# Attention with a relation bias and a mixture of experts: the relation part of the scores moved to 64-row tiles

## The chip, the cores and the metric

One core of a Trainium2 chip runs the kernel. The metric is device time in microseconds, the median of several runs; less is better.

## The reference, cut to what matters

One layer on 4096 tokens of width 256, 16 heads of width 16, then a mixture of 8 experts, two a token. The change is in the attention; its scores have an unusual term, a softmax over three relations for every pair of tokens, gated by the query.

```python
q, k, v = (x @ W.T + b).reshape(b, s, h, hd)          # for Wq, Wk, Wv
attn_scores = einsum('bihd,bjhd->bhij', q, k) / scale
logits = (x @ rel_W[:, :d].T)[:, :, None, :] + (x @ rel_W[:, d:].T)[:, None, :, :] + rel_b
relation_probs = softmax(logits, axis=-1)             # three relations per pair (i, j)
bias = einsum('bijk,hk->bhij', relation_probs, logical_bias)
gate = sigmoid(x @ gate_W.T + gate_b)                 # per query and head
attn_weights = softmax(attn_scores + gate * bias, axis=-1)
out = einsum('bhij,bjhd->bihd', attn_weights, v).reshape(b, s, d) @ Wo.T + bo
x = x + out
x = x + mixture_of_experts(layernorm(x))
```

## The kernel before, in words

Three parts run one after the other: `project_inputs` (layernorm, projections, the tables of the relation part, stored in device memory), `attend` (attention) and `experts`.

`attend` takes the queries in 32 chunks of 128 and the keys in 32 steps (`jt`) of 128; four steps are a unit (512 keys), eight units a chunk. Two of the three relation probabilities suffice, since the third is one less their sum. With the differences of the logits clamped, a probability is 1/(1 + e^a + e^b). A map of such probabilities for 128 queries and the 512 keys of a unit is made in a "turn", two turns a unit, 16 a chunk:

- VectorE adds key logits (`dj`) and query constants and clamps, two instructions a turn (`dve_d`, L726).
- ScalarE takes exponentials, two a turn (`act_r_exp`, L682), in even steps; then logarithm and exponential again (`act_r_inv`, L688 and L690), in odd steps.
- GpSimd adds the two exponentials between these (L636), and splits the result in a high and a low half-precision part (`pool_r`, L642 and L644). It works four turns ahead.
- SP copies the parts from 128 query rows into `rst`, where 16 queries lie on 16 rows and the 8 blocks of queries side by side (`sp_r`, L542): 3 parts of 64 queries each, twice a turn, so twelve copies of 64 KB a unit.

The product of `rst` (stationary, 112 rows: two maps of 16 queries in three parts, and 16 rows of ones) with `cm` (moving) adds gate times bias, less the row's bound, to the scores. `cm` is made by GpSimd for each chunk in two halves of heads, from the coefficients `cval` and a unit pattern `eye` (`pool_c`, L626, in the turns of `C_MAPS`). The row bounds in it come from the maxima: for each chunk TensorE multiplies queries and keys once more ahead of time (`pe_pair`, L835, 64 rows by 512 columns, two halves of the array), VectorE reduces each result (`dve_pair`, L734), and after the last of a chunk `dve_m` makes the bounds, which SP stores and loads again into `cval` (L556, L562).

TensorE's step, as its order is written in `chunk`: the scores of the next step in two halves of eight heads each (`pe_scores`: per half eight products of `kst` and `qm` over 128 rows, L814, and eight relation matmuls over 112 rows, L824), a pair of maxima, the weighted values of this step (`pe_pv`, L860), and a second pair of maxima. Each half of the scores waits until ScalarE has taken the exponential of the half before in the same banks (`p_ready`); ScalarE's two exponentials a step (L703) wait for `scores_ready`, one for each half. The maxima go to a ring of three banks and wait for VectorE (`mx_used`).

SP's order in a unit (`chunk` of the sync block): the copies of the next unit's maps, then the load of key logits four units ahead (`sp_dj`); in between at unit 0 the loads of `qm` (`sp_q`), at unit 1 those of `qx`, at unit 6 the bounds, at unit 7 the constants of the chunk after next (`sp_consts`, four loads).

Before, in `project_inputs`, SP stores `c_values` in 48 pieces (L213) ahead of the key logits (L217); ScalarE's copies of the key logits wait for these stores, and TensorE's value matmuls (L447) for ScalarE's copies. Loads of x and stores of the result are split in eight by blocks of queries (`by_block`).

## Time and profile before

| | |
|---|---|
| median of 3 runs | 5008.73 us (5006.49 to 5010.47) |
| the profiled execution, its own time | 5018.32 us |
| its span, first to last instruction | 5016.4 us |
| granted clock of TensorE, mean | 0.946 of 2.4 GHz |
| busy: TensorE, VectorE, ScalarE, GpSimd | 4458, 3822, 3381, 2057 us |

The span is a little shorter than the execution's own time, which has starting and ending around it. Busy times are sums over the three parts; what an engine does in the attention loop is read from a window of that loop. In the rows below, a line begins with its start in us from the span's start and its length, unless the heading says otherwise; "x8" counts instructions merged in a row, and brackets give idle time before it and what ended that.

### The profile page before, as it was taken

The numbers are of one execution on the slowest core, as the hardware profiler recorded it, in microseconds if no ns is written. First come the engines' busy times: TensorE is split into PE (matmuls) and PEld (weight loads), VectorE is DVE, ScalarE is ACT, GpSimd is POOL, SyncE is SP. The second block draws the span as 40 slices with busy tenths as digits, with TensorE's granted clock in tenths as the row PEclk, the third lists the DMA queues.
The fourth block names the chain that finished last, engine by engine and source line by source line (L and its number), as shares of the span: only waits on it lengthen the run. The fifth ranks groups of instructions, "written<-read, shape, count | busy, mean of one in ns | idle before, by whom it ended". The sixth has DMA issues, their size and how long they took to land. (4 is left out here: it accounts for less than half of the span.)

```text
span 5016.4 us, 183232 instructions
## 1 busy us (share of the span) xinstructions
PE 4458.2 (89%) x74128; PEld 3458.1 (69%) x74128; DVE 3821.7 (76%) x6309; ACT 3380.7 (67%) x4458; POOL 2057.0 (41%) x1809
## 2 busy tenths in 40 slices
PE   6459999999999999999999999999999996289992
PEld 3227777777777777777777777777777785267771
DVE  4388888888888888888888888888888843167773
ACT  2017887888787788877877787888888882044440
POOL 0114444444444444444444444444444442433335
PEclk9659999999999999999999999999999998589996
DMA  7514544544555445554454455454554456244434
GB/s 96 82 33 112 118 113 111 118 112 115 113 112 112 111 114 116 113 118 110 114 114 112 109 113 116 113 119 115 115 114 111 112 114 178 79 146 149 150 137 113
DMA packets 496919, 573.65 MB, mean 114 GB/s; under 512 B 136360, under 2 KB 369704, under 8 KB 492096
## 3 DMA queue, kind: packets, MB, share of 16 engines
q1 hardware_dynamic: 486880, 543.96, 46.5%
q0 software_dynamic: 6144, 16.79, 1.1%
q8 instruction: 600, 9.83, 0.9%
q14 instruction: 255, 2.09, 0.2%
q10 hardware_dynamic: 3040, 0.98, 0.1%
HBM read 305.10 MB, written 46.65 MB: 70 GB/s over the span
## 5 line engine op out<-in xcount | busy, mean ns | idle before, releaser
L734 DVE TENSOR_REDUCE b_mxp<-b_mx 128x1 f32<-128x512 f32 x4096 | 2635.4, 686 | 559.0 <-PE b_mx L835 508.9
L703 ACT ACTIVATE b_pr<-b_sc 128x1024 f32<-128x1024 f32 x2048 | 1986.5, 1021 | 697.0 <-PE b_sc L824 689.2
L814 PE MATMUL b_sc<-b_qm,kst 128*128 128x128 f16 x16384 | 1272.3, 220 | 54.3 <-ACT b_pr L703 42.0
L824 PE MATMUL b_sc<-b_cm,b_rst 112*128 112x128 f16 x16384 | 1264.5, 220 | 42.8 <-DMA b_rst<-b_rhi 35.5
L814 PEld LDWEIGHTS b_sc<-b_qm,kst 128*128 128x128 f16 x16384 | 971.6, 98 | 283.7 <-issue 229.5
L860 PE MATMUL b_acc<-b_pr,vp 128*32 128x128 f32 x32768 | 1124.1, 277 | 27.3 <-issue 26.9
L824 PEld LDWEIGHTS b_sc<-b_cm,b_rst 112*128 112x128 f16 x16384 | 1012.0, 98 | 49.4 <-DMA b_rst<-b_rhi 40.4
L860 PEld LDWEIGHTS b_acc<-b_pr,vp 128*32 128x32 f32 x32768 | 839.2, 110 | 265.2 <-ACT b_pr L703 190.2
L636 POOL TENSOR_TENSOR b_ex<-b_ex 128x512 f32<-128x512 f32 x512 | 654.7, 1279 | 680.8 <-ACT b_ex L682 680.8
L835 PE MATMUL b_mx<-kst,b_qx 64*128 64x512 f16 x4096 | 819.4, 397 | 92.1 <-DVE b_mxp L734 76.9
L642 POOL CAST b_rhi<-b_ex 128x512 f16<-128x512 f32 x512 | 312.8, 611 | 1293.0 <-ACT b_ex L690 1244.5
L726 DVE TENSOR_SCALAR b_dl<-b_dj,b_const 128x512 f32<-128x512 f32 x1024 | 671.9, 658 | 54.4 <-DMA b_dj<-key_logits 28.4
L644 POOL TENSOR_TENSOR b_rlo<-b_ex,b_rhi 128x512 f16<-128x512 f32 x512 | 628.1, 1227 | 41.0
L682 ACT ACTIVATE b_ex<-b_dl 128x512 f32<-128x512 f32 x1024 | 588.2, 630 | 14.6 <-DVE b_dl L726 14.6
L835 PEld LDWEIGHTS b_mx<-kst,b_qx 64*128 64x128 f16 x4096 | 197.5, 93 | 433.0 <-DVE b_mxp L734 303.5
L688 ACT ACTIVATE b_ex<-b_ex 128x512 f32<-128x512 f32 x512 | 323.4, 632 | 119.6 <-POOL b_ex L636 119.5
L690 ACT ACTIVATE b_ex<-b_ex 128x512 f32<-128x512 f32 x512 | 322.6, 630 | 16.2
L1324 ACT ACTIVATE c_h<-c_ps,c_b1b 128x512 f32<-128x512 f32 x184 | 126.6, 689 | 276.5 <-PE c_ps L1357 229.3
L1357 PE MATMUL c_ps<-c_xT,c_w1p 128*128 128x512 f16 x1104 | 258.1, 384 | 10.1 <-DVE c_xT L1194 10.0
L1368 PE MATMUL c_ps<-c_w2p,c_a 128*128 128x256 f16 x2208 | 255.4, 273 | 0.0
L1368 PEld LDWEIGHTS c_ps<-c_w2p,c_a 128*128 128x128 f16 x2208 | 216.0, 98 | 36.0
L1357 PEld LDWEIGHTS c_ps<-c_xT,c_w1p 128*128 128x128 f16 x1104 | 155.0, 145 | 87.5 <-issue 21.6
(144 smaller groups left out, 1726.0 us busy)
## 6 DMA issues: line engine op xcount, KB each, us to landing
b_dj<-key_logits SPq DMA_DIRECT2D x256, 768.0 KB, 7.9
b_rst<-b_rhi SPq DMA_DIRECT2D x2048, 64.0 KB, 3.2
b_rst<-b_rlo SPq DMA_DIRECT2D x1024, 64.0 KB, 3.1
c_w1r<-in_L_ffn_W_dram SPq DMA_DIRECT2D x23, 1024.0 KB, 4.9
c_w2r<-in_L_ffn_W_dram SPq DMA_DIRECT2D x23, 1024.0 KB, 4.8
expert_tokens<-c_zeros SPq DMA_DIRECT2D x23, 512.0 KB, 6.8
c_xb<-expert_tokens SPq DMA_DIRECT2D x23, 512.0 KB
expert_results<-c_y SPq DMA_DIRECT2D x23, 512.0 KB, 2.9
```

Source lines behind the costliest of these rows:

```text
L636: nc.gpsimd.tensor_tensor(ex[:, k, 0], ex[:, k, 0], ex[:, k, 1], ALU.add).then_inc(s["sum_ready"], 1)
L644: nc.gpsimd.tensor_tensor(rlo[:, slot], ex[:, k, 0], rhi[:, slot], ALU.subtract).then_inc(s["lo_ready"], 1)
L682: nc.scalar.activation(ex[:, k, i], dl[:, k, i], ACT.Exp, scale=sign).then_inc(s["e_ready"], 1)
L703: nc.scalar.activation(pr[:, jt % 2, half, :], sc[:, half].rearrange("p a b -> p (a b)"), ACT.Exp).then_inc(s["p_ready"], 1)
L726: nc.vector.tensor_scalar(dl[:, k, n], dj[:, u % 2, d], const[:, par, b:b + 1], limit, ALU.add, op).then_inc(s["d_ready"], 1)
L734: nc.vector.tensor_reduce(mxp[:, head, part:part + 1], mx[:, (bank + ab) % MX_RING, :], AX.X, ALU.max).then_inc(s["mx_used"], 1)
L814: pe.matmul(sc[:, half, side, p * P:p * P + P], kst[:, pair, jt * P:jt * P + P], qm[:, par, :, pair, side * IS:side * IS + IS], start=(p = ...
L824: ins = pe.matmul(out, rst[:, u % 2, b, j0:j0 + P], cm[:, par, half, b], start=False, stop=(b % (NB // 2) == NB // 2 - 1), skip_group_chec ...
L835: pe.matmul(mx[:, (bank + ab) % MX_RING, :], qx[rows, par, pair, :], kst[rows, pair, j0:j0 + 512], start=True, stop=True).then_inc(s["mx_r ...
L860: ins = pe.matmul(acc[32 * (h % 4):32 * (h % 4) + 32, h // 4, :], vp[:, jt, VW * h:VW * h + 32], pr[:, jt % 2, half].rearrange("p (a h i) ...
L1357: ins = pe.matmul(ps[:, n % 4, :], w1p[:, b % 2, wp, c, f:F:FT], xT[:, b % 2, xp, c], start=(c == 0 and wp == 0 and xp == 0), stop=(c == K ...
L1368: ins = pe.matmul(ps[:, 4 + d % 2, 0:D], hT[:, b % 2, hp, f, t * P:t * P + P], w2p[:, b % 2, wp, f, :], start=(f == 0 and hp == 0 and wp = ...
```

## The change

The relation part works on tiles of 64 rows. A map now has both probabilities of 64 queries (a "side"): the lower 64 partitions hold the first, the upper 64 the second. In `rst` each side has 64 rows: three parts of 16 neighbouring rows (two maps by 8 queries) and one of ones and zeros. A step's scores are now: relation matmuls of 64 rows and 64 columns, alternating between the two sides and thus the two halves of the array, for even heads and then for odd heads; then products of 64 rows and 64 columns, alternating between even and odd heads, in two turns. `scores_ready` comes twice at the end. ScalarE takes both exponentials of a turn in one instruction. Copies are six of 128 KB a unit, both sides one after the other; loads of `qm` move to unit 2, of `qx` to unit 3; maps are made a turn later, between GpSimd's sum and parts, and are half as long. Loading the constants takes eleven loads instead of four. Tokens lie in their natural order, so that x is loaded, and the result stored, in pieces eight times as large; `c_values` has another layout, with 4 stores instead of 48.

```diff
-NB, BI = 8, 16
+NB, BI = 8, 8
-C_MAPS = (12, 13)
+C_MAPS = (13, 14)
...
-            for part, t in ((0, chi), (1, chi), (2, clo)):
+            for part, t in enumerate((chi, clo)):
                 for k in range(2):
-                    for b in range(NB):
-                        sp.dma_start(c_dram[:, part, k].rearrange("x (i b) h -> b i x h", b=NB)[b],
-                                     t[BI * b:BI * b + BI, k]).then_inc(stored, 16)
+                    sp.dma_start(c_dram[part].rearrange("a k i x h -> k a i (x h)")[k],
+                                 t[:, k].rearrange("p x h -> p (x h)")).then_inc(stored, 16)
...
+        def sp_r(sp, x, u, side, parts):
+            if 0 in parts:
+                sp.wait_ge(s["lo_ready"], 16 * x + 2 * u + side + 1)
+                waited(sp)
+            for part in parts:
+                t = rlo if part == 1 else rhi
+                sp.dma_start(rst[IS * side + 16 * part:IS * side + 16 * part + 16, u % 2],
+                             t[:, 2 * (u % 2) + side, :]).then_inc(s[f"r_in{u % 2}"], 16)
...
                     for turn in range(2 * UNITS):
...
-                        pool_r(pool, c, g)
+                        pool_sum(pool, c, g)
                     if turn in C_MAPS and not last:
                         pool_c(pool, c + 1, 1 - par, nth + par, C_MAPS.index(turn))
+                    if g < 2 * UNITS:
+                        pool_parts(pool, c, g)
...
-            for i, sign in enumerate(((1.0, 1.0), (-1.0, 1.0))[k]):
-                nc.scalar.activation(ex[:, k, i], dl[:, k, i], ACT.Exp, scale=sign).then_inc(s["e_ready"], 1)
+            nc.scalar.activation(ex[:, k].rearrange("p n j -> p (n j)"), dl[:, k].rearrange("p n j -> p (n j)"),
+                                 ACT.Exp).then_inc(s["e_ready"], 1)
...
+        def pe_relation(pe, c, par, jt, half):
+            u, j0 = jt // 4, jt % 4 * P
             if jt == 0:
                 pe.wait_ge(s["c_made"], 2 * c + half + 1)
             if jt % 4 == 0 and half == 0:
-                pe.wait_ge(s[f"r_in{u % 2}"], 192 * (UNITS // 2 * c + u // 2 + 1))
+                pe.wait_ge(s[f"r_in{u % 2}"], 96 * (UNITS // 2 * c + u // 2 + 1))
+            if not (isinstance(c, int) and c == 0 and jt == 0):
+                pe.wait_ge(s["p_ready"], STEPS * c + 2 * jt + half - 1)
             for b in range(NB):
+                for side in range(2):
+                    rows = slice(IS * side, IS * side + IS)
+                    out = sc[:, half, side, :].rearrange("p (h i) -> p h i", h=PAIRS)[:, :, b * BI:b * BI + BI]
+                    ins = pe.matmul(out, rst[rows, u % 2, b, j0:j0 + P], cm[rows, par, half, b], start=(b == 0), stop=False,
+                                    skip_group_check=True)
+            return ins
+
+        def pe_products(pe, c, par, jt):
+            if jt == 0:
+                pe.wait_ge(s["q_in"], 64 * c + 64)
+            for turn in range(2):
+                if turn:
+                    pe.wait_ge(s["relation_done"], NT * c + jt + 1)
+                for pair in range(PAIRS):
+                    for ab in range(2):
+                        side, rows = (turn + ab) % 2, slice(64 * ab, 64 * ab + 64)
+                        ins = pe.matmul(sc[:, ab, side, pair * IS:pair * IS + IS], kst[rows, pair, jt * P:jt * P + P],
+                                        qm[rows, par, pair, side * IS:side * IS + IS], start=False,
+                                        stop=(pair == PAIRS - 1), skip_group_check=True)
+                        if pair == PAIRS - 1 and turn == 1:
+                            ins.then_inc(s["scores_ready"], 1)
...
-                for b in range(NB):
-                    sp.dma_start(by_block(out)[b // 4, b % 4, :, t, :], x1[BI * b:BI * b + BI, t, :]).then_inc(s["stored"], 16)
+                sp.dma_start(out.rearrange("o (t p) d -> (o p) t d", p=P)[:, t, :], x1[:, t, :]).then_inc(s["stored"], 16)
```

How instructions move, at three places. TensorE, the second step of a chunk (step 1 of the loop's first chunk; `b_sc` holds scores, `b_mx` maxima, `b_acc` weighted values). Before:

```order
L814 MATMUL b_sc<-b_qm,kst 128x128 [waits b_p_ready]
L814 MATMUL b_sc<-b_qm,kst 128x128 x7
L824 MATMUL b_sc<-b_cm,b_rst 128x8x16 x8
L810 REGISTER_ALU
L814 MATMUL b_sc<-b_qm,kst 128x128 [waits b_p_ready]
L814 MATMUL b_sc<-b_qm,kst 128x128 x7
L824 MATMUL b_sc<-b_cm,b_rst 128x8x16 x8
L844 REGISTER_ALU
L835 MATMUL b_mx<-kst,b_qx 128x512 [waits b_mx_used]
L835 MATMUL b_mx<-kst,b_qx 128x512
```

The same place now:

```order
L814 MATMUL b_sc<-b_cm,b_rst 128x8x8 [waits b_p_ready]
L814 MATMUL b_sc<-b_cm,b_rst 128x8x8 x15
L809 REGISTER_ALU
L814 MATMUL b_sc<-b_cm,b_rst 128x8x8 [waits b_p_ready]
L814 MATMUL b_sc<-b_cm,b_rst 128x8x8 x15
L828 MATMUL b_sc<-b_qm,kst 128x64 x16
L824 REGISTER_ALU
L828 MATMUL b_sc<-b_qm,kst 128x64 [waits b_relation_done]
L828 MATMUL b_sc<-b_qm,kst 128x64 x15
```

A half was complete after its own sixteen matmuls; now both halves are complete only after all 64, and the wait for the second exponential stands ahead of 48 of them.

SP, a chunk's unit 0 (`b_rst` the stacked maps, `b_qm` queries, `b_dj` key logits). Before, from the end of the first turn's copies to the start of the second's:

```order
L542 DMA b_rst<-b_rlo 16x4x512
L542 DMA b_rst<-b_rhi 16x4x512
L509 ISA
L509 DMA b_qm<-q_parts 32x1x1024
L509 ISA
L509 DMA b_qm<-q_parts 32x1x1024
L509 ISA
L509 DMA b_qm<-q_parts 32x1x1024
L509 ISA
L509 DMA b_qm<-q_parts 32x1x1024
L537 REGISTER_ALU
L542 DMA b_rst<-b_rhi 16x4x512 [waits b_lo_ready]
```

Now, from the first turn's copies to the key logits:

```order
L531 DMA b_rst<-b_rhi 16x8x512 [waits b_lo_ready]
L531 DMA b_rst<-b_rlo 16x8x512
L531 DMA b_rst<-b_rhi 16x8x512
L527 REGISTER_ALU
L531 DMA b_rst<-b_rhi 16x8x512 [waits b_lo_ready]
L531 DMA b_rst<-b_rlo 16x8x512
L531 DMA b_rst<-b_rhi 16x8x512
L591 ISA
L507 DMA b_dj<-key_logits 128x1x1024 [waits b_d_ready]
L580 REGISTER_ALU
```

The loads of queries stood between the two turns' copies and are gone from here; the copies are half as many.

GpSimd, the turn in which a chunk's first map (`b_cm`) is made. Before:

```order
L636 TENSOR_TENSOR b_ex<-b_ex 128x512 [waits b_e_ready]
L637 REGISTER_ALU
L639 ISA [waits b_r_ready]
L642 CAST b_rhi<-b_ex 128x512 [waits b_r_in0]
L644 TENSOR_TENSOR b_rlo<-b_ex,b_rhi 128x512 [waits b_hi_ready]
L622 ISA
L623 ISA [waits b_cval_in1]
L625 REGISTER_ALU [waits b_m_in]
L626 TENSOR_TENSOR b_cm<-b_cval,b_eye 112x1024 [waits b_scores_ready]
L635 ISA
L636 TENSOR_TENSOR b_ex<-b_ex 128x512 [waits b_e_ready]
```

Now:

```order
L626 TENSOR_TENSOR b_ex<-b_ex 128x512 [waits b_e_ready]
L613 ISA
L614 ISA [waits b_cval_in1]
L616 REGISTER_ALU [waits b_m_in]
L617 TENSOR_TENSOR b_cm<-b_cval,b_eye 128x512 [waits b_scores_ready]
L636 CAST b_rhi<-b_ex 128x512 [waits b_r_ready,b_r_in0]
L638 TENSOR_TENSOR b_rlo<-b_ex,b_rhi 128x512 [waits b_hi_ready]
L625 REGISTER_ALU
L626 TENSOR_TENSOR b_ex<-b_ex 128x512 [waits b_e_ready]
L617 TENSOR_TENSOR b_cm<-b_cval,b_eye 128x512
L636 CAST b_rhi<-b_ex 128x512 [waits b_r_ready,b_r_in1]
L638 TENSOR_TENSOR b_rlo<-b_ex,b_rhi 128x512 [waits b_hi_ready]
```

The map stood behind the parts (L642, L644) of its turn and in front of the next turn's sum (L636); it now stands between the sum (L626) and the parts (L636, L638) of a turn, one turn later.

## Rows read from the trace of the kernel before

**Rows 1.** The page, part 1: span, busy time, share and count by engine.
```profile
span 5016.4 us, 183232 instructions
PE 4458.2 (89%) x74128; PEld 3458.1 (69%) x74128; DVE 3821.7 (76%) x6309; ACT 3380.7 (67%) x4458; POOL 2057.0 (41%) x1809
```

**Rows 2.** Stretches: window, its length, busy PE, PEld, DVE, ACT, POOL, clock, DMA, GB/s.
```profile
359.00:4170.00 3811.00, 3675.13 (x69536) 2891.80 (x69534) 3158.49 (x5106) 3084.59 (x4076) 1701.35 (x1586) 0.99 0.50 113
260.00:350.00 90.00, 39.45 (x130) 6.78 (x130) 83.61 (x132) 0.00 (x0) 3.77 (x2) 0.50 0.02 3
1000.00:3000.00 2000.00, 1927.78 (x36253) 1510.20 (x36252) 1697.75 (x2745) 1611.16 (x2130) 894.60 (x833) 0.99 0.50 113
```

**Rows 3.** Timeline of TensorE, one undisturbed step.
```profile
2004.30 0.62 PE L814 MATMUL b_sc<-b_qm,kst 128*128 128x128 f16 x8
...
2005.66 0.61 PE L824 MATMUL b_sc<-b_cm,b_rst 112*128 112x128 f16 x8
2006.20 0.39 PE L835 MATMUL b_mx<-kst,b_qx 64*128 64x512 f16 x2
2006.52 1.08 PE L860 MATMUL b_acc<-b_pr,vp 128*32 128x128 f32 x32
2007.53 0.39 PE L835 MATMUL b_mx<-kst,b_qx 64*128 64x512 f16 x2
2007.86 0.23 PE L814 MATMUL b_sc<-b_qm,kst 128*128 128x128 f16 x1
```

**Rows 4.** Waits in 1000 to 3000: us in total, times, longest.
```profile
POOL b_cm L626 <- DMA b_cval<-row_bounds: 61.5, 17, 4.7
...
PE b_acc L860 <- issue: 12.7, 15, 2.0
```

**Rows 5.** Timeline at a chunk's first unit, TensorE and SP.
```profile
2049.76 0.45 PE L824 MATMUL b_sc<-b_cm,b_rst 112*128 112x128 f16 x5 [0.82 <-DMA b_rst<-b_rhi]
2043.86 1.23 SPq L542 DMA_DIRECT2D b_rst<-b_rhi  x2
```

**Rows 6.** Timeline of TensorE, maxima before the loop.
```profile
300.53 0.61 PE L835 MATMUL b_mx<-kst,b_qx 64*128 64x512 f16 x2 [0.78 <-DVE b_mxp L734]
```

**Rows 7.** Timeline of ScalarE and VectorE in undisturbed steps.
```profile
2005.41 1.94 ACT L703 ACTIVATE b_pr<-b_sc 128x1024 f32<-128x1024 f32 x2 [0.43 <-PE b_sc L824]
2007.23 1.15 ACT L682 ACTIVATE b_ex<-b_dl 128x512 f32<-128x512 f32 x2
2039.38 2.62 DVE L734 TENSOR_REDUCE b_mxp<-b_mx 128x1 f32<-128x512 f32 x4
2041.92 0.50 DVE L726 TENSOR_SCALAR b_dl<-b_dj,b_const 128x512 f32<-128x512 f32 x1
```

**Rows 8.** The page, part 6: DMA issues, KB each, median us to landing.
```profile
b_dj<-key_logits SPq DMA_DIRECT2D x256, 768.0 KB, 7.9
b_rst<-b_rhi SPq DMA_DIRECT2D x2048, 64.0 KB, 3.2
```

**Rows 9.** Timeline of SP, constants at the start of the attention.
```profile
226.47 1.25 SPq L529 DMA_DIRECT2D b_const<-query_consts  x2
```

**Rows 10.** Timeline of SP and TensorE in the projections.
```profile
161.98 22.31 SPq L213 DMA_DIRECT2D c_values<-a_chi  x32
184.34 8.43 SPq L213 DMA_DIRECT2D c_values<-a_clo  x16
...
194.99 5.49 PE L447 MATMUL a_ps<-a_wv,a_xnT 128*128 128x256 f32 x12 [44.10 <-ACT a_dj L384]
```

**Rows 11.** Timeline of VectorE and SP at the end.
```profile
5007.83 1.67 DVE L1287 SCALAR_TENSOR_TENSOR c_x<-c_a,c_pw,c_x 128x256 f32<-128x256 f32 x4
4994.38 19.97 SPq L1074 DMA_DIRECT2D out_dram<-c_x  x20
```

**Rows 12.** Timeline of TensorE in the last chunk, which has no maxima.
```profile
4162.39 1.08 PE L860 MATMUL b_acc<-b_pr,vp 128*32 128x128 f32 x32
...
4165.30 1.08 PE L860 MATMUL b_acc<-b_pr,vp 128*32 128x128 f32 x32
```

**Rows 13.** The page, part 3: DMA queue, packets, MB, share of 16 engines.
```profile
q8 instruction: 600, 9.83, 0.9%
```

More of the change, by code:

```diff
@@ L33 @@
 HH = H // 2
-NB, BI = 8, 16
+NB, BI = 8, 8
 IS = P // 2
+PARTS = 4
 JU = 512
@@ L51 @@
 EXP_MAX = 43.0
-M_ROW = 6 * BI
-ROWS = M_ROW + BI
 MXU = S // 512
@@ new lines, in sp_consts @@
+                for k in range(2):
+                    sp.dma_start(const[IS * k:IS * k + IS, par, side],
+                                 const_dram[bass.ds(x, 1)].rearrange("o (s b i) n -> (o s) i b n", s=2, b=NB)[side, :, :, 2 * k:2 * k + 2]
+                                 ).then_inc(s[f"const_in{par}"], 16)
+            sp.dma_start(bound[:, par],
+                         const_dram[bass.ds(x, 1)].rearrange("o p n -> (o p) n")[:, 4:4 + H]).then_inc(s[f"const_in{par}"], 16)
+        def sp_r(sp, x, u, side, parts):
[6 more added lines that the diff above has]
+                             t[:, 2 * (u % 2) + side, :]).then_inc(s[f"r_in{u % 2}"], 16)
@@ L578, in _ @@
                 sp_dj(sp, u)
-            for k in range(2):
-                sp_r(sp, 0, 0, k)
+            sp.wait_ge(s["ones_made"], 1)
+            for side in range(2):
+                sp_r(sp, 0, 0, side, range(3))
             sp_m_out(sp, 0)
@@ L588, in chunk @@
                     waited(sp)
-                    for k in range(2):
+                    for side in range(2):
                         if u + 1 < UNITS:
-                            sp_r(sp, c, u + 1, k)
+                            sp_r(sp, c, u + 1, side, range(3))
                         elif not last:
-                            sp_r(sp, c + 1, 0, k)
-                        if u == 0 and k == 0 and not last:
-                            sp_q(sp, c + 1, 1 - par)
-                        if u == M_UNIT and not last:
-                            if k == 0:
-                                sp_m_out(sp, c + 1)
-                            else:
-                                sp_m_in(sp, c + 1, 1 - par)
+                            sp_r(sp, c + 1, 0, side, range(3))
+                    if u == M_UNIT and not last:
+                        sp_m_out(sp, c + 1)
+                        sp_m_in(sp, c + 1, 1 - par)
                     if u + 4 < UNITS or not last:
@@ L606, in chunk @@
                         sp_att(sp, c)
-                        if more:
-                            sp.wait_ge(s["c_made"], 2 * c + 2)
-                            waited(sp)
-                            sp_qx(sp, c + 2, par)
+                    if u == 2 and not last:
+                        sp_q(sp, c + 1, 1 - par, qm, "q_in")
+                    if u == 3 and more:
+                        sp.wait_ge(s["c_made"], 2 * c + 2)
+                        waited(sp)
+                        sp_q(sp, c + 2, par, qx, f"qx_in{par}")
                     if u + 1 == UNITS and more:
@@ L801, in _ @@
             dve_out(dve, NT)
-        def pe_scores(pe, c, par, jt, half):
+        def pe_relation(pe, c, par, jt, half):
             u, j0 = jt // 4, jt % 4 * P
-            if jt == 0 and half == 0:
-                pe.wait_ge(s["q_in"], 64 * c + 64)
-            if not (isinstance(c, int) and c == 0 and jt == 0):
-                pe.wait_ge(s["p_ready"], STEPS * c + 2 * jt + half - 1)
-            for p in range(4):
-                pair = 4 * half + p
-                for side in range(2):
-                    pe.matmul(sc[:, half, side, p * P:p * P + P], kst[:, pair, jt * P:jt * P + P],
-                              qm[:, par, :, pair, side * IS:side * IS + IS], start=(p == 0), stop=False,
-                              skip_group_check=True)
             if jt == 0:
@@ L855, in pe_pv @@
                 pe.wait_ge(s["acc_read"], c + 1)
[L856 to L862 removed]
+            pe.wait_ge(s["p_ready"], STEPS * c + 2 * jt + 2)
+            for h in range(H):
+                ins = pe.matmul(acc[32 * (h % 4):32 * (h % 4) + 32, h // 4, :], vp[:, jt, VW * h:VW * h + 32],
+                                pr[:, jt % 2, h % 2].rearrange("p (a h i) -> p h a i", a=2, h=PAIRS)[:, h // 2],
+                                start=(jt == 0 and h < 4), stop=(jt == NT - 1), skip_group_check=True)
             ins.then_inc(s["pv_done"], 1)
@@ L881, in _ @@
             pe.wait_ge(s["ones_made"], 1)
-            for half in range(2):
-                pe_scores(pe, 0, 0, 0, half)
+            pe_scores(pe, 0, 0, 0)
             def chunk(c, par, nth, last):
```

191 lines of the change are left out of this document (84 added, 107 removed).

## The prediction, made before the changed kernel was run

> **What bounds the kernel now.** I read the page's first part for the span and the stretches by window for where the time lies: the attention loop, from the first to the last row of L860, takes 3811 of 5016.4 us [rows 1, 2]. In its middle 2000 us ScalarE ran 2130 instructions; a step has two L703 and, on average, two of the others, so these are 532.5 steps of 3.756 us. Per step TensorE is busy 1928/532.5 = 3.62 us, VectorE 3.19, ScalarE 3.03, GpSimd 1.68. TensorE is the bound, VectorE 15% behind it.
>
> Then the timeline of one undisturbed step [rows 3]: scores begin at 2004.30 and again at 2007.86, a period of 3.56 us without a gap. The first 24 of the 32 score matmuls take 2005.66 - 2004.30 = 1.36 us, 57 ns each; the fourth block to the next maxima takes 0.54 where a block takes 0.45; each pair of maxima 0.32 to its successor, the 32 of L860 1.01. So a mean step loses 3.756 - 3.56 = 0.20 us to disturbances. The waits name some: GpSimd waits 61.5 us for the row bounds before it makes a map; TensorE waits for a late copy of L542 at a chunk's first unit (0.82 us here, in the middle of the scores); and 12.7 us stand as "issue", in 15 stops between matmuls of L860 [rows 4, 5].
>
> **The change, part by part.**
>
> *Scores.* 32 matmuls of 128 columns become 64 of 64 columns, one after another in opposite 64-row halves of the array and in different banks. No row shows such a short pair. Two rows show that halves run side by side: with the clock at half speed (0.50 granted in 260 to 350, that is 1.2 GHz) the two L835 of a pair, 512 columns each, are done together in 0.61 us [rows 2, 6], where 1024 columns in a row alone need 0.85; in the loop (2.4 GHz, 0.99) both take 0.39 where a row of 1024 needs 0.43 [rows 3]. A 128-column matmul is 53 ns of columns and 3 to 4 more. Low bound for a pair of 64: 27 + 3 = 30 ns. High bound: both keep today's 57, one behind the other, 114 ns. Between lies 60, short but not side by side. I take 30, since the L835 rows are of the same shape of tile. Then scores cost 32 x 30 = 0.96 us instead of 1.82.
>
> *Changes of tile shape.* Score, maxima and score again now share the 64-row shape. The 0.09 us lost between the last relation block and the maxima and the 0.32 - 0.22 = 0.10 between maxima and scores (512 columns at 2.4 GHz are 0.21, and the second starts just behind) [rows 3] go; those around L860 stay. TensorE's step: 0.96 + 0.22 + 0.32 + 1.01 = 2.51 us. It is the bound no longer.
>
> *The chain that is new.* Both halves of a step now become ready together, and the second half's relation needs both exponentials of the step before. So this runs in series, once a step: two L703 (1.94 us, [rows 7]), a hand-over before and one behind them (0.04 each: the relation block of [rows 3] ends at 4.76 + 0.61 = 5.37, L703 starts at 5.41), 8 + 16 pairs, and the last matmul's own 0.22 (0.61 less seven times 57 ns). At 30 ns a pair this is 1.94 + 0.08 + 0.72 + 0.22 = 2.96 us. The new wait for relation_done stands in the middle of the products, behind 8 pairs (0.24 us) issued after the last relation matmul (0.22): 0 to 0.05 us. Queued behind these waits are the maxima, so VectorE waits if the chain is late; at 3.0 us it is not.
>
> *ScalarE.* Two exponentials of 512 (1.15 us together) become one of 1024. Nearest row: two of 1024 in 1.94, 0.97 each [rows 7]. ScalarE falls to some 2.95 us a step, under VectorE.
>
> *VectorE* keeps all its work: four reductions, 2.54 us from the first to the clamp [rows 7], a clamp and the chunk's small work, 3.19 us a step in all. **This becomes the bound.** Its reductions need TensorE to fill the ring of three banks; with 2.51 us of work a step TensorE has 0.7 us to spare.
>
> *Copies and SP's queue.* Twelve issues a unit of about 0.6 us become six of twice the size, moved ahead of the loads of queries, which go to units 2 and 3. Price of one: 0.6 (as now) to 1.2 us (as two now), so 3.7 to 7.4 us, and 3.2 us to land [rows 5, 8]: within a unit of 4 x 3.29 = 13 us. The late copy at a chunk's first unit goes. At the last unit the constants take 11 issues instead of 4, at 0.63 us [rows 9] 6.9 us; with the copies and one of L522 that is 11 to 15 us of 13, which moves the next copies by 2 us at most and still lets them land in time. Cost nothing, at most 2 x 32 = 64 us. The key logits fall from 768 to 512 KB a unit.
>
> *Maps.* Half as large, two turns of GpSimd's stay, a turn later and between sum and parts, where GpSimd waits for ScalarE anyway. The 61.5 us wait for the bounds and what it delays go.
>
> *Before the loop.* 48 stores of c_values (30.7 us of SP, 161.98 to 192.8) become 4, 2.5 us by their own issue time; behind them the stores of key logits are queued, and TensorE waits 44 us for these [rows 10]. That is 28 us off. At the start of attention 16 more small loads stand ahead of the key logits, 16 x 0.63 = 10 us on. The 32 loads of x become 4; I count nothing for them.
>
> *Behind the loop.* The last 8 stores follow the last result (5009.5) until 5014.4 [rows 11]; one store instead saves 4 us.
>
> **The sum.** A step: 3.19 plus half of today's 0.20 for disturbances that are not named above (they hit TensorE, which now has slack, but come at a faster pace) = 3.29 us. The last 32 steps have no maxima: 4165.30 - 4162.39 = 2.91 us each [rows 12], 93 us. So the other 992 now take (3811 - 93)/992 = 3.75. Gain: 992 x 0.46 = 456 us, less 32 x 0.05 = 2 in the last chunk; 28 - 10 + 4 = 22 outside. Together 476 us. The profiled execution took 5018.32 us around its span, 9.6 over the median of 5008.73; I subtract from the median: **4533 us**. With no disturbances at all (3.19): 4431. With 3.45 a step: 5008.7 - 298 + 2 - 22 = 4691.
>
> **The rivals.**
>
> *Instructions do not come fast enough* (0.12). The 600 fetches of 9.83 MB [rows 13] are 16 KB each, and TensorE has most of the 183,232 instructions. The change adds 32,768 matmuls and as many loads to its 148,000, in less time: a fetch every 4 us instead of 6. The stops of [rows 4] speak for it; that they are few speaks against. If the mean step is 3.5: 992 x 0.25 = 248, with the 20 outside 4741 us; the band is 4690 to 4800.
>
> *Halves not side by side* (0.09). The serial chain is the place: 2.24 + 48 x the price of a matmul. At 30 ns each it is 3.68, with 0.1 of disturbances 3.78; 992 x 0.03 + 32 x 0.77 - 22 = 33 us more, 5042 us. It decides from 29 ns a matmul on: above that the kernel is slower. For it: the short matmuls accumulate, the L835 do not. Against: [rows 6]. A third of its chance I give to faster, a little to no change.
>
> *The clock* (0.04). In 260 to 350, where TensorE was busy 44% of the time, 1.2 GHz was granted; in the loop, at 96%, 2.4 GHz [rows 2]. The new loop would lie between, at 2.5/3.29 = 76%. If half the steps ran at the lower level (2.5 becomes 4.9), the mean is 4.1: some 330 us slower, 5340.
>
> *A matmul keeps its price of 57 ns* (0.02). Chain 2.24 + 48 x 0.057 = 4.98, step 5.08: 992 x 1.33 + 32 x 2.07 - 22 = 1360 more, 6370 us. Against: L860's 32 take 1.01 us, 32 ns each [rows 3].
> The Trainium skill ("TensorE: Matmul & The Clock Gate", section "Wait — 56ns, not 53.3ns?") has a rule of this kind: with hardware decode off a matmul costs the sequencer about 62 ns, which binds once the array needs less. By it the 100 matmuls of a step would take an estimated 6.2 us; the 32 ns of L860 do not agree with it, so the measurement decides.
>
> *The change does not do what it says* (0.01): time as before less the 22.
>
> **How the numbers follow.** The main case has 0.72 and reaches from 4431 to 4691. With most of the first rival, to 4760, it holds 8 in 10. A measurement here can tell 0.2% (10 us) from no change. Faster: 0.72 + 0.12 + 0.03 = 0.87; the same: 0.02; slower: 0.05 + 0.04 + 0.02 = 0.11.
>
> **What would show it.** Right: the period of an undisturbed step is 3.1 to 3.3 us with VectorE busy over 93% in the loop, pairs of 64-column matmuls start together and 16 pairs last about 0.5 us, L447 waits some 16 us instead of 44, no wait of a map for row bounds. Wrong: ScalarE waiting for the products each step while VectorE idles (halves not side by side), "issue" stops many times more numerous (fetches), a granted clock under 0.95 in the loop.

## The result: 13.6% slower, and the profile after

The changed kernel takes **5685.15 us** (median of 4 runs, 5680.37 to 5687.63) where the kernel before, run beside it, takes 5007.61 (4 runs, 4995.95 to 5010.47): a ratio of **1.136** (95% interval 1.134 to 1.138). The forecast was 4533 us, range 4430 to 4760. The sign is wrong and the miss is 1152 us. Of the four runs of one kernel below, that with the split maxima, one fell in a slower state of the chip (5310 us against 5158 to 5176); its number is the median of the other three.

The page of the kernel after, part 1, the clock row of part 2 and two rows of part 5 (busy us, mean ns of one | idle time before them and what ended it); part 1 answers to [rows 1].

```profile
span 5682.0 us, 247181 instructions
PE 3885.5 (68%) x106896; PEld 2877.1 (51%) x106896; DVE 3735.3 (66%) x6310; ACT 3326.3 (59%) x3946; POOL 2005.4 (35%) x1816
...
PEclk8578888888888888888888888888888888769996
...
L814 PE MATMUL b_sc<-b_cm,b_rst 64*128 64x64 f16 x32768 | 810.1, 200 | 781.8 <-DMA b_rst<-b_rhi 657.4
...
L723 DVE TENSOR_SCALAR b_dl<-b_dj,b_const 128x512 f32<-128x512 f32 x1024 | 661.0, 648 | 512.0 <-DMA b_dj<-key_logits 508.7
```

TensorE fell from 4458 us of work to 3886, as it was meant to, and no engine is busy over 68%. What is new is idle time that ends with a transfer: the first relation matmul of a unit (L814) waits 657 us for the copies of the maps' parts into `rst` (called tails from here on), the clamps (L723) 509 us for the key logits.

Stretches of the kernel after, the whole loop and its middle (window, length, busy PE, PEld, DVE, ACT, POOL, clock, DMA share, GB/s), which answer to [rows 2]:

```profile
340.00:4852.00 4512.00, 3098.01 (x102218) 2306.53 (x102210) 3072.53 (x5106) 3029.63 (x3568) 1652.52 (x1585) 0.87 0.33 82
1000.00:3000.00 2000.00, 1376.29 (x45090) 1020.06 (x45082) 1399.34 (x2323) 1338.81 (x1578) 733.54 (x704) 0.87 0.33 82
```

From the first to the last weighted sum the loop grew from 3811 to 4513 us, 702 more; outside it 36 us were saved (20 before it, 16 behind it). 702 - 36 is the 666 us by which the spans differ. The DMA engines look idler than before, 0.33 against 0.50. That is the trap in this case: the share is a mean over 16 engines.

One late unit, the timeline of TensorE, then SP's queue, then VectorE in the kernel after:

```profile
2513.40 0.63 PE L814 MATMUL b_sc<-b_cm,b_rst 64*128 64x64 f16 x32
2513.87 0.69 PE L828 MATMUL b_sc<-b_qm,kst 64*128 64x64 f16 x32
2514.40 0.38 PE L847 MATMUL b_mx<-kst,b_qx 64*128 64x512 f16 x2
2514.71 1.08 PE L870 MATMUL b_acc<-b_pr,vp 128*32 128x128 f32 x32
...
2516.16 0.95 PE L814 MATMUL b_sc<-b_cm,b_rst 64*128 64x64 f16 x32
...
2523.99 0.39 PE L847 MATMUL b_mx<-kst,b_qx 64*128 64x512 f16 x2 [1.14 <-DVE b_mxp L731]
2529.86 0.34 PE L814 MATMUL b_sc<-b_cm,b_rst 64*128 64x64 f16 x6 [5.47 <-DMA b_rst<-b_rhi]
```

```profile
2503.48 0.56 SPq L507 DMA_DIRECT2D b_dj<-key_logits  x1
2504.16 9.45 SPq L502 DMA_DIRECT2D b_qm<-q_parts  x4
2513.93 2.15 SPq L531 DMA_DIRECT2D b_rst<-b_rhi  x1
...
2520.08 2.57 SPq L531 DMA_DIRECT2D b_rst<-b_rhi  x1
```

```profile
2515.20 2.48 DVE L731 TENSOR_REDUCE b_mxp<-b_mx 128x1 f32<-128x512 f32 x4
2517.59 0.48 DVE L723 TENSOR_SCALAR b_dl<-b_dj,b_const 128x512 f32<-128x512 f32 x1
2517.98 2.48 DVE L731 TENSOR_REDUCE b_mxp<-b_mx 128x1 f32<-128x512 f32 x4
2522.85 0.48 DVE L723 TENSOR_SCALAR b_dl<-b_dj,b_const 128x512 f32<-128x512 f32 x1 [2.39 <-DMA b_dj<-key_logits]
```

Where nothing is late a step can last 2516.16 - 2513.40 = 2.76 us, better than the 3.2 forecast; the median of all steps but those in which a unit begins is 3.02. The first step of the next unit starts 5.5 us late, for its tails. SP's issues have become slow as well: 9.45 us for 4 loads of queries, 2.4 each, where the kernel before took 3.03 us for the four. After the issue of L507, the view of the DMA engines in the ten microseconds from 2503 (busy share of all 16 in tenths, 40 slices):

```profile
DMA  0140101101011111111111110110401101111011
```

The pieces behind this row, from the records of the same trace, in which a load of key logits is 128 pieces of 4096 bytes (pieces that start in each microsecond / pieces in flight, in the mean):

```
2509   4096 B: 12 / 2.0
2510   4096 B: 14 / 2.1
2511   4096 B: 12 / 2.0
2517   4096 B: 8 / 2.0    1024 B (tails): 178 / 10.5
2525   2048 B (queries): 25 / 2.1
2527   2048 B (queries): 4 / 0.4    1024 B (tails): 40 / 1.8
2528   4096 B: 3 / 0.4    1024 B (tails): 36 / 1.7
```

**The load of key logits is on 2 engines of 16.** The records don't name engines; they show two pieces at a time. Between 1000 and 3000 us such pieces are in flight for 1517 us, 1.94 at a time in the mean, and more than two for only 68 us. In the kernel before the same load (384 pieces of 2048 bytes) had 8.7 pieces in flight in the mean. The last rows show who stands behind it: of the 768 pieces of the unit's six tail copies, 672 had started by 2525, and the last 96, which are two sixteenths, come from 2526 on, two at a time, behind the pieces of the queries. The matmul that needs them starts at 2529.86. The source of the changed load is `[2, 64, 1024]`: two different rows, each repeated for 64 partitions, so its outermost dimension is 2. Before it was one row repeated for 128.

The Trainium skill ("DMA: Bandwidth & Descriptors", section "Why a DMA increments its semaphore by 16 and not by 1") states the rule: the number of engines is the largest up to 16 that divides the outermost dimension (of more than one) of both sides, and on SP's queue they are the lowest-numbered ones. The trace agrees on the number, with 1.94 pieces in flight in the mean; which engines they are it can't show. The Trainium skill ("DMA: Bandwidth & Descriptors", section "Rules for kernel authors") warns that an outermost dimension under 16 holds the whole transfer to that many engines, with a leading broadcast as its example; here the two rows are different ones, and the two pieces at a time are the same. The prediction did not weigh this rule.

### The profile page after: what moved, and what is told of

Read it like the earlier page. It is cut to its first block and busy times, and to the rows that moved or that the text cites. A ratio compares the mean times of both kernels' runs of the same rounds, so it can differ in the third digit from the quotient of the medians.

```text
span 5682.0 us, 247181 instructions
## 1 busy us (share of the span) xinstructions
PE 3885.5 (68%) x106896; PEld 2877.1 (51%) x106896; DVE 3735.3 (66%) x6310; ACT 3326.3 (59%) x3946; POOL 2005.4 (35%) x1816
## 5 line engine op out<-in xcount | busy, mean ns | idle before, releaser
L731 DVE TENSOR_REDUCE b_mxp<-b_mx 128x1 f32<-128x512 f32 x4096 | 2580.5, 681 | 895.6 <-PE b_mx L847 873.8
L814 PE MATMUL b_sc<-b_cm,b_rst 64*128 64x64 f16 x32768 | 810.1, 200 | 781.8 <-DMA b_rst<-b_rhi 657.4
L847 PE MATMUL b_mx<-kst,b_qx 64*128 64x512 f16 x4096 | 879.7, 424 | 640.2 <-DVE b_mxp L731 621.9
L870 PE MATMUL b_acc<-b_pr,vp 128*32 128x128 f32 x32768 | 1251.6, 296 | 33.4 <-issue 31.5
L626 POOL TENSOR_TENSOR b_ex<-b_ex 128x512 f32<-128x512 f32 x512 | 664.9, 1299 | 1557.3 <-ACT b_ex L681 1556.2
L814 PEld LDWEIGHTS b_sc<-b_cm,b_rst 64*128 64x128 f16 x32768 | 702.2, 101 | 996.1 <-issue 765.4
L870 PEld LDWEIGHTS b_acc<-b_pr,vp 128*32 128x32 f32 x32768 | 925.9, 118 | 331.6 <-issue 309.6
L723 DVE TENSOR_SCALAR b_dl<-b_dj,b_const 128x512 f32<-128x512 f32 x1024 | 661.0, 648 | 512.0 <-DMA b_dj<-key_logits 508.7
L828 PE MATMUL b_sc<-b_qm,kst 64*128 64x64 f16 x32768 | 746.4, 199 | 50.2 <-issue 49.2
L636 POOL CAST b_rhi<-b_ex 128x512 f16<-128x512 f32 x512 | 321.4, 628 | 1139.6 <-ACT b_ex L690 1035.2
L828 PEld LDWEIGHTS b_sc<-b_qm,kst 64*128 64x128 f16 x32768 | 635.6, 101 | 58.2 <-issue 56.9
L638 POOL TENSOR_TENSOR b_rlo<-b_ex,b_rhi 128x512 f16<-128x512 f32 x512 | 615.9, 1203 | 40.9
L681 ACT ACTIVATE b_ex<-b_dl 128x1024 f32<-128x1024 f32 x512 | 541.5, 1058 | 29.4 <-DVE b_dl L723 29.4
L1208 DVE TENSOR_TENSOR c_a<-c_h,c_a 128x512 f16<-128x512 f32 x184 | 210.2, 1143 | 6.3
```

Source lines behind the costliest of these rows:

```text
L626: nc.gpsimd.tensor_tensor(ex[:, g % 2, 0], ex[:, g % 2, 0], ex[:, g % 2, 1], ALU.add).then_inc(s["sum_ready"], 1)
L638: nc.gpsimd.tensor_tensor(rlo[:, slot], ex[:, g % 2, 0], rhi[:, slot], ALU.subtract).then_inc(s["lo_ready"], 1)
L681: nc.scalar.activation(ex[:, k].rearrange("p n j -> p (n j)"), dl[:, k].rearrange("p n j -> p (n j)"), ACT.Exp).then_inc(s["e_ready"], 1)
L723: nc.vector.tensor_scalar(dl[:, side, n], dj[:, u % 2, n], const[:, par, side, n:n + 1], EXP_MAX, ALU.add, ALU.min).then_inc(s["d_ready"], 1)
L731: nc.vector.tensor_reduce(mxp[:, head, part:part + 1], mx[:, (bank + ab) % MX_RING, :], AX.X, ALU.max).then_inc(s["mx_used"], 1)
L814: ins = pe.matmul(out, rst[rows, u % 2, b, j0:j0 + P], cm[rows, par, half, b], start=(b == 0), stop=False, skip_group_check=True)
```

## The experiments

**Theory 1**: the load on two engines fills them, and the parts of the tail copies, and the loads of queries (32 rows as 2 times 16, two engines in both kernels), queue behind it there. The rivals: six copies of 128 KB at once are late by themselves (2); the loads of queries, moved to units 2 and 3, do the harm (3); the serial chain is slow (4). Four kernels on one chip, beside the kernel before at 5011.72 us. The edits shown from here on are shortened; "..." stands for what is left out, and counts that waits need with them are not shown.

*Key logits in two loads.*

```
-sp.dma_start(dj[:, u % 2].rearrange("p n j -> p (n j)"),
-             dj_dram[u].rearrange("(k n) j -> k (n j)", k=2).unsqueeze(1).broadcast_to([2, IS, 2 * JU])) ...
+for k in range(2):
+    sp.dma_start(dj[IS * k:IS * k + IS, u % 2], dj_dram[u, 2 * k:2 * k + 2].partition_broadcast(IS)) ...
```

> The changed kernel, the load of the key logits alone written as two loads, one for each 64 partitions. Theory 1 (the one load, whose outermost dimension is 2, is carried by 2 of the 16 DMA engines for some 8.5 us, and the copies of the tails to those engines' rows queue behind it): the tails arrive in time, steps 3, 7, 11, 15, 19, 23, 27 and 31 of a chunk fall from 4 to 13 us to 3 to 4 us, some 31 to 39 us a chunk, and the total is 4450 to 4700 us. Theory 2 (six copies of 128 KB each issued at once are themselves late): no change beyond 1%, 5630 to 5740 us. Theory 3 (the loads of queries in units 2 and 3 do the harm): steps 15 and 19 stay over 9 us, the total falls by at most half, 5200 to 5450 us. Theory 4 (the serial chain of exponentials and products is slow in itself): no change, the clamps and the tails were late only beside it.

Measured: **4837.09 us** (4831 to 4844), ratio 0.965 (0.963 to 0.968). The load alone takes off 848 us and makes the change faster than the kernel before. The tails are no longer waited for. Waits in 1000 to 3000 (us in total, times, longest) of the changed kernel, and of this one:

```profile
PE b_sc L814 <- DMA b_rst<-b_rhi: 287.7, 101, 9.1
...
DVE b_dl L723 <- DMA b_dj<-key_logits: 190.4, 85, 7.5
...
POOL b_cm L617 <- DMA b_cval<-row_bounds: 56.3, 11, 7.6
...
PE b_sc L828 <- issue: 20.9, 35, 1.5
...
PE b_sc L814 <- issue: 16.2, 24, 2.4
PE b_acc L870 <- issue: 14.0, 20, 2.1
```

```profile
POOL b_rhi L637 <- DMA b_rst<-b_rhi: 183.1, 76, 4.7
...
PE b_sc L815 <- issue: 103.2, 111, 3.8
PE b_sc L829 <- issue: 98.7, 109, 2.1
...
PE b_acc L871 <- issue: 53.2, 62, 2.2
...
PE b_sc L815 <- DMA b_rst<-b_rhi: 0.6, 1, 0.6
```

The median length of steps over the 32 chunks, by their number in a chunk (from the ends of the weighted sums in the traces), shows which ones were late. Ahead of the sums of steps 3, 7 and so on stand the scores of the next step, with which a unit begins:

```
step                     3      7     11     15     19     23     27     31    all, mean
before                  4.71   3.55   3.55   3.55   3.55   3.55   3.55   3.55    3.72
changed                 8.30   4.54   7.25  11.79  13.26   3.97   4.90  10.21    4.41
key logits in two       3.72   4.01   3.78   3.61   3.84   3.57   4.46   3.53    3.60
queries only            8.37   4.62   6.84   7.50   9.61   4.23   4.20  10.56    4.18
before, two engines    14.08   7.81  15.19   7.95   9.33   9.07   8.17  10.28    5.26
```

Theories 2 and 4 fall: the six copies and the chain are as they were. The total is 137 us above the range of theory 1; what holds the step at 3.60 is asked below.

*Queries on 16 rows a load as well.*

```
-sp.dma_start(t[row:row + 32, par] ..., parts_twice(x, ab, part)) ...
+for copy in range(2):
+    sp.dma_start(t[row + 16 * copy:row + 16 * copy + 16, par] ..., q_dram[bass.ds(x, 1), ab, part] ...) ...
```

> As the kernel with the key logits in two loads, and each load of queries for 32 rows (outermost dimension 2) written as two loads of 16 rows. Theory 1: the last loads that use 2 engines are gone; against the kernel with the key logits alone mended another 0 to 4 us a chunk at steps 15 and 19, total 4400 to 4650 us, 0 to 130 us below it. Eight more issues of some 0.6 us a unit in units 2 and 3 could cost SP 5 us there; if SP is then late the gain is gone, total up to 50 us above it. Theory 3: this kernel, and not the other, brings the steps 15 and 19 down, by 18 us a chunk, 560 us below the other.

Measured: 4864.9 us, ratio 0.973 (0.970 to 0.976): 28 us above the kernel with the key logits alone and 215 above the range, so the gain that was expected is not there. Steps 15 and 19 stand at 3.85 and 3.67 us, where they were 3.61 and 3.84 without this edit. Once the two engines are no longer full, the queries' loads on them cost nothing that shows. Whether the 28 us are the 8 issues a chunk more was not looked into.

*Queries alone mended* (the second edit without the first).

> The changed kernel, the loads of queries alone mended (two of 16 rows for one of 32), the key logits as they were. Theory 1: the key logits still hold 2 engines 8.5 us a unit, so steps 3, 7, 11, 23, 27, 31 stay at 4 to 10 us; steps 15 and 19 fall to the 5 to 8 us of their neighbours, 8 to 14 us a chunk, total 5250 to 5450 us. Theory 3: steps 15 and 19 fall to 3 to 4 us and take the others with them, total under 5000 us. Theory 2: 5630 to 5740 us.

Measured: 5440.0 us, ratio 1.086 (1.084 to 1.089). Steps 15 and 19 fall by 4.3 and 3.7 us, as theory 1 said; of the others 27 falls by 0.7 and the rest move by some 0.4 at most. Theory 3 falls as the main cause; the queries' own share is some 245 us, and only while the key logits fill the same engines.

*The kernel before, with nothing but its load of key logits on two engines.*

```
-sp.dma_start(dj[:, u % 2], dj_dram[:, u * JU:u * JU + JU].partition_broadcast(P)) ...
+sp.dma_start(dj[:, u % 2] ..., dj_dram[:, u].unsqueeze(1).broadcast_to([2, IS, 3 * JU])) ...
```

> The kernel before, its key logits kept twice in DRAM so that the one load of 128 partitions has an outermost dimension of 2 (128 pieces of 6 KB; the order of the work, the copies, the tiles are as before; eight small stores more ahead of the loop). Theory 1: the load takes 2 engines some 13 us of a unit's 15, the copies queue behind it, the loop is held by it: total 5400 to 6400 us. Any theory that puts the loss to the copies, the order of issues or the tiles: the load still lands a unit before its clamp, total 4990 to 5050 us.

Measured: 6598.84 us, ratio **1.318** (1.315 to 1.321), more than the range. The copies, tiles and order of work are those of the kernel before, and its undisturbed steps are still 3.55; those in which a unit begins take 8 to 15 us. Its load is half as large again as the changed kernel's (128 pieces of 6 KB), so the price is not the same, but the cause is. This settles the cause apart from everything else in the change.

**What holds the mended kernel at 3.60 us a step?** The forecast was 3.29. Its TensorE stops in the middle of a row of matmuls with "issue", that is, waiting for nothing that the profile shows: above, 98.7 us at L829 (the products) where the changed kernel had 20.9 at the same place (L828). In 2000 us there are 484 pauses of over 0.35 us between two matmuls of one line, 388 us together. Of these 209 (93 us) stand ahead of the second half of the relation matmuls, which waits for an exponential; the other 275 are called stops from here on. They take 295 us, 0.53 us a step; the kernel before has 23, 25 us or 0.05 a step. That was the first rival of the prediction. The fetches of TensorE's instructions are 16 KB each, and this kernel's 446 in 2000 us brought 113,476 instructions, 254 each. Its stretch (columns as above) and its fetches there (number, MB, share of 16 engines):

```profile
1000.00:3000.00 2000.00, 1583.97 (x55252) 1174.37 (x55243) 1728.55 (x2845) 1636.03 (x1931) 913.00 (x863) 0.97 0.44 100
...
q8 instruction: 446, 7.31, 1.8%
```

The times of the fetches tie the stops to them. 96% of the 275 stops end 1.1 to 1.8 us after a fetch has landed, though a fetch lands only every 4.5 us in the mean, so that chance would put 16% there. Nor does VectorE hold this kernel: its last chunk has no maxima and so little for VectorE, and its steps still last 3.56 us in the median (2.99 in the changed kernel).

Theory F: instructions do not come fast enough. P: TensorE's own work is the bound. S: the serial chain is. All edits from here on are on the mended kernel, where nothing else is said.

```
-for pair in range(PAIRS):
+for pair in range(PAIRS // 2):
 ...
```

> On the kernel with the key logits in two loads (4837 us, 3.60 us a step, 484 stops between matmuls of one line in 2000 us that wait for nothing but 'issue'): products of 4 of the 8 pairs only, so 32 of some 205 instructions of a step on TensorE fall and 0.24 us of its work; the exponential is taken with scale 0, its time unchanged. The scores of half the heads are left out. Theory F (instructions are fetched 256 at a time every 4.5 us, and this holds the step): 173 instructions at 57 per us are 3.03 us, so the step falls to VectorE's 3.15 to 3.3, total 4490 to 4640 us, and the stops with 'issue' fall to under half. Theory P (TensorE's own work holds the step): 0.24 us less, 4590 us. Theory S (the chain of exponentials, hand-over, products): 0.12 us less, 4715 us. F and P are told apart by the next kernel.

Measured: 4588.11 us, ratio to before 0.915 (0.913 to 0.917), 3.35 us a step; the stops fall to 163, or 0.25 us a step. That is as much as F or P wants and twice what S allows; the stops halved in time, but not in number.

```
-acc[32 * (h % 4):32 * (h % 4) + 32, h // 4, :], ... pr[:, jt % 2, h % 2] ... [:, h // 2]
+acc[32 * (h % 4):32 * (h % 4) + 32, h // 4, 0:IS], ... pr[:, jt % 2, h % 2] ... [:, h // 2, 0]
```

> On the same kernel: the weighted sums over values for 64 of the 128 queries only, so that each of these 32 matmuls of a step has 64 columns in place of 128; half of the attention output is left out. The instructions are the same in number, TensorE has some 0.45 us less work a step. Theory F: no gain, since as many instructions are fetched and they are wanted faster: 4760 to 4880 us, with more 'issue' stops. Theory P: 0.45 us less a step, 4340 to 4450 us. Theory S: no change either, 4800 to 4860 us, but with no more 'issue' stops than in the kernel it is based on.

Measured: 4832.34 us, ratio 0.964 (0.961 to 0.967), 3.58 us a step, with 294 stops, 0.57 us a step. TensorE's work in 1000 to 3000 fell from 1584 to 1418 us and the time stayed. P falls.

*More instructions for the same columns.*

```
-for ab in range(2):  ... matmul(mx[..., :], qx[rows, par, pair, :], kst[rows, pair, j0:j0 + 512] ...)
+for piece in range(4):
+    for ab in range(2):  ... matmul(mx[..., P * piece:P * piece + P], qx[rows, par, pair, :], kst[rows, pair, j0 + P * piece:j0 + P * piece + P] ...)
```

> On the kernel with the key logits in two loads (4837 us, 3.60 us a step): each of the 4 matmuls for maxima of a step, 512 columns, as four of 128 columns, so 24 instructions of a step more (12 matmuls, 12 loads of weights; 229 in place of 205) for the same columns. TensorE's own work grows by 12 times some 4 ns, 0.05 us. Theory F (instructions are fetched too slowly for this step): 12% more to fetch, the step grows by 0.2 to 0.43 us, total 5030 to 5280 us, stops with 'issue' as many or more. Any theory by which TensorE, VectorE or the serial chain holds the step by its work: at most 0.1 us a step, 4830 to 4940 us.

Measured: 5169.20 us, ratio 1.034 (1.031 to 1.037), 3.92 us a step, 363 stops, 0.90 us a step. 24 small instructions cost 0.32 us where their own work is 0.05, and the stops alone grew by 0.37. F holds, and S, which the kernel with half the weighted sums left standing, falls.

*Semaphore increments instead.*

```
 ins.then_inc(s["pv_done"], 1)
+for n in range(16):  pe.sem_inc(s["pe_idle"], 1)
```

> On the same kernel: 16 increments of a semaphore that nobody waits for, on TensorE behind each step's weighted sums. Theory F: 221 instructions a step in place of 205, the step 8% longer where the fetches hold it, 3.88 us, total 5050 to 5150 us, and 8% more fetches. Theory S and any theory in which TensorE has 0.7 us a step to spare: under 1% more, 4800 to 4890 us. A price of the increments themselves of over 40 ns each would look like F in the total; then the stops with 'issue' are no more numerous.

Measured: 5694.01 us. This was a bad probe: the increments themselves cost 0.11 us each. The stretch behind the weighted sums in its timeline:

```profile
2005.40 1.08 PE L871 MATMUL b_acc<-b_pr,vp 128*32 128x128 f32 x32
2008.23 0.39 PE L848 MATMUL b_mx<-kst,b_qx 64*128 64x512 f16 x2 [1.76 <-DVE b_mxp L732]
```

2008.23 - 2005.40 is 2.83 us, of which the sums take 1.01; that leaves 1.82 us for 16. "<-DVE" in the row is misleading: VectorE's last reduction had ended 0.64 us before. At 4.3 us in most steps 6 stops are left of 275, so the fetches do keep up with a slower pace.

*Is it the fetches' own pace, or the traffic beside them?*

```
-dj[IS * k:IS * k + IS, u % 2]            -rst[..., u % 2]
+dj[IS * k:IS * k + IS, u % 2, :, cols]   +rst[..., u % 2, :, 0:JU // 2]
 ...     with cols = 0:JU // 2 from u = 2 on
```

> On the kernel with the key logits in two loads (4837 us): the loads of key logits (after the first two) and the six copies of tails a unit move 256 of the 512 columns only, so half the bytes of the loop's traffic with as many issues; the relation of the other keys is left out. Theory F-own (the fetch of instructions has its own pace, whatever else the DMA engines carry): 4780 to 4850 us, a fetch still lands some 1.25 us after its start and the stops with 'issue' stay. Theory F-shared (the fetches stand behind this traffic in the same engines): a fetch takes 0.9 to 1.1 us, the stops fall by a third or more, the total falls to 4600 to 4750 us. If neither holds and late copies still cost something, GpSimd's wait for the copies (183 us in 2000) falls and the total falls by under 60 us.

Measured: 4589.14 us, ratio 0.920 (0.915 to 0.925), 3.34 us a step, 11 us under the range of F-shared. A fetch takes 1.09 us in the median where it took 1.25, and the stops fall from 0.53 to 0.29 us a step (236 of 173 us). Its stretch (columns as above), and its waits there:

```profile
1000.00:3000.00 2000.00, 1653.35 (x59448) 1236.18 (x59442) 1875.45 (x3062) 1764.04 (x2079) 990.53 (x928) 1.00 0.25 65
...
POOL b_rhi L638 <- DMA b_rst<-b_rhi: 117.3, 57, 4.0
...
PE b_sc L816 <- issue: 55.8, 93, 3.4
...
PE b_sc L830 <- issue: 49.2, 99, 1.2
```

Theory F-shared fits best: the fetches get through sooner when less stands beside them. The 0.24 us that the stops lost are nearly the 0.26 us that the step lost. But GpSimd's wait for the copies fell too, from 183 to 117 us, and the granted clock rose from 0.97 to 1.00, so some of the gain may be from there. Here VectorE is busy 1875 of 2000 us, 94%, as it is in the kernel with half the products: where the stops are short, the bound that the prediction named is close.

*Weights and values in float16*, one matmul of the weighted sums in place of two, on the mended kernel and on the kernel before:

```
-pr = sb("pr", [P, 2, 2, PAIRS * P])          -vp: sbuf_tensor("vp", [P, NT, VPAD], F32)
+pr = sb("pr", [P, 2, 2, PAIRS * P], F16)     +vp: sbuf_tensor("vp", [P, NT, VPAD], F16)
```

> On the same kernel: weights and values of the weighted sums in float16 in place of float32, so that a head's sum is one matmul in place of two: 32 instructions and some 0.5 us of TensorE's work a step less. Theory F: 173 instructions a step, the step falls to VectorE's 3.15 to 3.3 us, total 4490 to 4640 us, a candidate to beat both kernels. Theory P: the same or less, 4320 to 4450 us where ScalarE writing half the bytes helps too. Theory S: within 1% of 4837 us.

Measured: **4773.45 us**, ratio 0.951 (0.949 to 0.954), the fastest complete kernel here and faster than both. But it is 3.52 us a step, 133 us above F's range. 191 stops are left, 0.34 us a step, and in 1000 to 3000 the granted clock was 0.90 (0.97 in the mended kernel): less work on TensorE, and longer stretches at the lower level.

> The kernel before with weights and values of the weighted sums in float16: TensorE loses 32 of 143 instructions and 0.5 us of work a step, the scores stay as they were (64 instructions where the change has 128). TensorE's step becomes 3.05 us, VectorE's 3.19 is then the bound, as in the changed kernel with the loads mended. Theory F: at 111 instructions a step the fetches keep up, the step is 3.25 to 3.4 us, total 4610 to 4720 us, with few 'issue' stops, below the changed kernel in every form run so far but the one that leaves products out. If instead VectorE, ScalarE or their hand-overs hold a step at 3.5 to 3.6 us whatever TensorE does, this kernel ends at 4780 to 4900 us too.

Measured: 4908.31 us, ratio 0.983 (0.980 to 0.986). 5 stops are left, as F said, and yet the total is 188 us above its range. Another bound stands there, a handshake, in its TensorE timeline:

```profile
2007.49 0.61 PE L824 MATMUL b_sc<-b_cm,b_rst 112*128 112x128 f16 x8
2008.03 0.39 PE L835 MATMUL b_mx<-kst,b_qx 64*128 64x512 f16 x2
2008.35 0.41 PE L860 MATMUL b_acc<-b_pr,vp 128*32 128x128 f16 x16
2009.20 0.39 PE L835 MATMUL b_mx<-kst,b_qx 64*128 64x512 f16 x2 [0.44 <-DVE b_mxp L734]
2009.53 0.62 PE L814 MATMUL b_sc<-b_qm,kst 128*128 128x128 f16 x8
```

TensorE waits for VectorE to free a bank of maxima, then writes scores while VectorE waits for the next ones (248 and 244 us of such waits in 1000 to 3000): 3.39 us in most steps.

*Is the alternation of halves what makes the short matmuls cheap?*

```
-for b in range(NB):  for side in range(2):     -for pair in range(PAIRS):  for ab in range(2):
+for side in range(2):  for b in range(NB):     +for ab in range(2):  for pair in range(PAIRS):
```

> On the kernel with the key logits in two loads: the same matmuls of 64 columns in another order, all of one 64-row half and then all of the other, so that neighbours are in the same half. If only the alternation makes two matmuls cost 29 ns, the 64 now take 29 to 57 ns each, 0.9 to 2.7 us a step more on TensorE and 0.7 to 2 us more on the serial chain: step 4.3 to 5.8 us, total 5500 to 7100 us. If matmuls of one half follow each other at 29 ns for two as well (64 columns are 27 ns of columns), no change but for the stops, 4780 to 4900 us. Theory F adds nothing here: the instructions are as many.

Measured: 4846.02 us, ratio 0.969 (0.967 to 0.971), as much as with alternation. A relation block of 29 matmuls then takes 0.96 us, 27 ns a matmul, where 32 alternated take 0.63, 14 ns. So halves do run side by side, and without it a score block would still follow at the pace of its columns. TensorE has 0.2 us a step more work and the time stays, against P and S once more. The added work fills idle time: the 209 pauses ahead of the second half of the relation fall to 3, and the stops from 0.53 to 0.40 us a step.

## Why the prediction was wrong, point by point

- **The step that failed is "Copies and SP's queue", with its "Cost nothing, at most 2 x 32 = 64 us".** It priced the issues and counted the bytes, with "The key logits fall from 768 to 512 KB a unit" as relief. It did not ask over how many engines a load is spread. The load mended, 848 us return; the same load in the kernel before costs 1587 us (6598.84 - 5011.72).
- *Halves side by side, 30 ns a pair*: right. Alternated matmuls take 14 ns each, and the scores of the step shown above 2514.40 - 2513.40 = 1.00 us, 0.96 forecast.
- *VectorE is the bound at 3.19*: the work was sized about right, but it did not bind. It is busy 1728.55/555 = 3.11 us a step in the mended kernel. Where nothing disturbs it, its period is 2517.98 - 2515.20 = 2.78 us, but a third of the mended kernel's clamps last over 0.6 us instead of 0.48. Busy share in the changed kernel's loop was 68% (3072.53/4512), not over 93%, and 86% in the mended one.
- *The serial chain, 2.96 us*: right, and not what the loss came from. The last chunk, which has no maxima, shows it nearly bare, with 2.99 us a step in the median.
- *Instructions do not come fast enough* (0.12, 4741 us): the second cause. It holds the mended kernel at 3.60 us where 3.29 was forecast: 1023 x 0.31 = 317 us, against 4837 - 4533 = 304. The price forecast for it, 3.5 us a step, was near; the chance was too small. That the bursts, 128 instructions in one microsecond of scores, make it so, where the mean of a fetch every 4 us looked harmless, is our reading and not shown. The Trainium skill ("Runtime: NRT & Kernel Launch", section "Instruction fetch mechanics") calls the refill mostly hidden; here it is not, by the 275 stops.
- *The clock*: the sign named in the prediction, under 0.95, came (0.87), with TensorE at 3098/4512 = 69% and long waits at the units. It is 0.97 once the waits go, so it was mostly a consequence. What share of the loss it carried was not measured alone.
- *A price of 57 ns a matmul* and *the change does not do what it says*: wrong, by the same rows.
- *Maps*: the wait for row bounds did not go (56.3 us, [rows 4] had 61.5) while the queue was full. In the mended kernel it is not among the waits.
- *Before the loop*: the values' first late matmul (L447 before, L439 now) waits 19.6 us, some 16 were forecast; the loop starts 20 us earlier, 18 forecast. *Behind it* 16 us instead of 4; where the other 12 come from stays open.
- Two slips of the working change nothing: VectorE's 3.19 us is 12% behind TensorE's 3.62, not 15%, and the bound of 4431 us leaves out the 2 us of the last chunk that the bound of 4691 has.

## What to carry to other kernels

For every transfer that a change rewrites, write down the outermost dimension of both sides before anything else: bytes and issues may fall while the transfer becomes several times slower, and the mean DMA share falls too, which looks like relief. Here the transfer on two engines also delayed the other transfers that had a part on these engines, and SP's issues behind it. And when an engine's work is cut into more and shorter instructions, price their fetches too, in the burst and not only in the mean over a step, together with the traffic beside them.

## What the runs showed of the hardware that was not expected

- A load on two engines started 12 to 14 pieces of 4096 bytes in a microsecond, some 52 KB, when hardly anything else was in flight, and the issue of a load of queries behind it took SP 2.4 us.
- A fetch of 16 KB brought 254 of TensorE's instructions, and a stop ended 1.1 to 1.8 us after a fetch had landed (96% of 275 stops of the mended kernel).
- With half the bytes in the loop's other transfers, and as many issues, a fetch of instructions took 1.09 us instead of 1.25.
- An increment of a semaphore on TensorE's queue cost 0.11 us, as much as eight of the short matmuls side by side.
- The granted clock, a mean over stretches at 2.4 and 1.2 GHz, was 0.97 in the mended kernel with TensorE busy 1584 us of 2000, and 0.90 with the float16 sums and 1340 us of 2000.
